# Using the shared product form for the last two missing taps of an input block, and moving VectorE's differences ahead of two groups of additions

## The reference, cut to what matters

```python
# x: (8, 64, 128, 64) = B, C, T, V float32
xp = jnp.pad(x, ((0, 0), (0, 0), (0, 8), (0, 0)), mode='edge')   # time
patches = xp[:, :, idx, :]                 # 16 patches of 16 steps, stride 8
xf = jnp.fft.rfft(patches, axis=-2, norm='ortho')
h = concat(real, imag) @ W.T               # 8 * 64 * 16 = 8192 tokens of 64
...
f = l2norm(h)
attn = softmax(f @ f.T)                    # 8192 x 8192
h = layernorm(h + l2norm(0.8 * f + 0.2 * attn @ f))
h = layernorm(h + moe_top2_of_8(h))        # exact gelu experts
```

## Time and profile before

| | |
|---|---|
| time, median of 3 runs | 855.12 us (854.82 to 855.29) |
| profiled execution: its time, its span | 855.08 us, 853.0 us |
| PE busy | 838.5 us (98%) |
| DVE busy | 781.0 us (92%) |
| ACT busy | 660.0 us (77%) |
| POOL busy | 184.8 us (22%) |
| DMA | 26.09 MB, mean 31 GB/s |

### The profile page before, as it was taken

One profiled execution on the slowest core, in us unless ns is written; L12 is line 12 of the kernel. 1 busy time (PEld: TensorE's weight loads), 2 busy tenths in 40 slices (PEclk: granted clock), 3 DMA queues, 4 the chain that ended last, 5 costly groups with the idle time before them and its releaser, 6 DMA issues.

```text
span 853.0 us, 31799 instructions
## 1 busy us (share of the span) xinstructions
PE 838.5 (98%) x13818; PEld 431.9 (51%) x13818; DVE 781.0 (92%) x920; ACT 660.0 (77%) x1312; POOL 184.8 (22%) x191
## 2 busy tenths in 40 slices
PE   9999999999999999999999999999999999999995
PEld 6444556755555555555555555555555555543331
DVE  4888999999999999999999998999989999999994
ACT  0368888888888888888888888888888888977873
POOL 1275910000400000000000000000000299948323
PEclk9999999999999999999999999999999999999998
DMA  9982150000000000000000000000000000000111
GB/s 297 348 219 59 27 91 3 3 2 2 3 3 3 3 2 3 2 3 2 2 3 2 3 3 3 3 2 3 3 2 3 3 3 3 3 2 2 39 26 37
DMA packets 31578, 26.09 MB, mean 31 GB/s; under 512 B 12552, under 2 KB 29456, under 8 KB 31440
## 3 DMA queue, kind: packets, MB, share of 16 engines
q1 hardware_dynamic: 22912, 15.54, 7.5%
q10 hardware_dynamic: 8464, 8.52, 3.2%
q0 software_dynamic: 64, 0.01, 0.0%
HBM read 17.77 MB, written 2.10 MB: 23 GB/s over the span
## 4 chain that ended last, share of the span: by engine, by line
PE 89%; DVE 6%; DMA 2%; issue 2%; ACT 1%; POOLq 0%; DVEq 0%; POOL 0%; ACTq 0%
PE ps L565 37%; PE ps L582 26%; PE ps L595 12%; PE ps L668 3%; PE ps L752 3%; DVE ring L1101 3%; DMA big<-in_x_dram 2%; PE ps L609 1%; PE ps L473 1%; PE ps L681 1%; PE ps L487 1%; PE ps L767 1%; PE ps L449 0%; DVE ring L1266 0%; DVE sums L1060 0%
## 5 line engine op out<-in xcount | busy, mean ns | idle before, releaser
L1101 DVE TENSOR_TENSOR ring<-ring 128x1024 f16<-128x1024 f32 x512 | 605.0, 1233 | 33.1 <-ACT ring L974 32.1
L974 ACT ACTIVATE ring<-ps 128x1024 f32<-128x1024 f32 x512 | 519.7, 1021 | 120.7 <-PE ps L565 120.5
L565 PE MATMUL ps<-big 64*64 64x512 f16 x6144 | 376.1, 375 | 1.3 <-ACT ring L974 0.9
L582 PE MATMUL ps<-ring,both_f 64*64 64x512 bf16 x4096 | 275.1, 384 | 0.0
L565 PEld LDWEIGHTS ps<-big 64*64 64x64 f16 x6144 | 176.6, 106 | 160.3 <-ACT ring L974 5.5
L582 PEld LDWEIGHTS ps<-ring,both_f 64*64 64x64 f16 x4096 | 119.3, 106 | 106.6
L595 PE MATMUL ps<-ring,both_f 64*64 64x512 f16 x2048 | 154.3, 376 | 0.1
L974 ACT ACTIVATION_READ_ACCUMULATOR ring<-ps 128x1 f32 x512 | 101.3, 198 | 0.0
L393 POOL TENSOR_SCALAR stat<-stat 128x16 f32<-128x16 f32 (+2 forms) x4 | 2.9, 723 | 444.0 <-DVE stat L1150 443.7
L595 PEld LDWEIGHTS ps<-ring,both_f 64*64 64x64 f16 x2048 | 59.8, 107 | 51.8 <-issue 1.9
L937 ACT ACTIVATE ring<-ps,b1s 128x512 f32<-128x512 f32 x64 | 40.4, 683 | 16.7 <-PE ps L668 16.6
(11 more groups left out here) (193 smaller groups left out, 550.4 us busy)
## 6 DMA issues: line engine op xcount, KB each, us to landing
ring<-in_x_dram ACTq DMA_DIRECT2D x6, 1024.0 KB, 15.4
ring<-in_x_dram SPq DMA_DIRECT2D x6, 1024.0 KB, 21.7
big<-big SPq DMA_DIRECT2D x16, 128.0 KB, 2.4
out_dram<-h SPq DMA_DIRECT2D x14, 128.0 KB, 2.4
both_f<-in_x_dram ACTq DMA_DIRECT2D x1, 1024.0 KB, 22.0
both_f<-in_x_dram SPq DMA_DIRECT2D x1, 1024.0 KB, 22.3
big<-in_x_dram SPq DMA_DIRECT2D x1, 1024.0 KB, 24.1
big<-in_x_dram ACTq DMA_DIRECT2D x1, 1024.0 KB, 14.6
```

The costliest lines, as they stand in the source:

```text
L565: last = mm(bank(SLOT_BANK[slot_of(s)] + r)[m:m + 64, :], of_k[r][:, 128 * k + m:128 * k + m + 64], of_q[r][:, q0 + 512 * r:q0 + 512 * r + ...
L582: last = mm(bank(sums_bank(s // NT) + half)[m:m + 64, :], fs[64 * r:64 * r + 64, s % NT, m:m + 64], probs[64 * r:64 * r + 64, s % 8, :].bi ...
L974: a(probs[:, s % 8, :], bank(SLOT_BANK[slot_of(s)], 2), ACT.Exp, accum_out=rowsum[:, s:s + 1]).then_inc(s_pr, 1)
L1101: tt(probs_lo[:, s % 8, :], probs[:, s % 8, :], probs[:, s % 8, :].bitcast(BF16)[:, 1:2 * QC:2], ALU.subtract).then_inc(s_lo, 1)
```

## The change

Blocks 6 and 7 use the shared form in tap 0 too, as blocks 1 to 5 do. In DVE's loop, for `b = 7` all four differences come before `tokens_out(4)` and `tokens_out(5)`, which now follow each other; for `b = 3` and `b = 5` the order is what it was. `norms(4)` follows `tokens_out(5)`.

```diff
-SHARED_TAPS = [()] + 5 * [(0, 1, 2, 3)] + 2 * [(1, 2, 3)]
+SHARED_TAPS = [()] + 7 * [(0, 1, 2, 3)]
...
             for b in (3, 5, 7):
                 taps = SHARED_TAPS[b]
-                for s in taps[:-2]:
+                ahead = 2 if b < B - 1 else len(taps)
+                for s in taps[:ahead]:
                     differences_of(b, s)
                 tokens_out(b - 3)
-                differences_of(b, taps[-2])
+                for s in taps[ahead:-1]:
+                    differences_of(b, s)
                 tokens_out(b - 2)
-                differences_of(b, taps[-1])
+                if b < B - 1:
+                    differences_of(b, taps[-1])
                 norms(b - 3)
                 if b < B - 1:
                     taps = SHARED_TAPS[b + 1]
                     differences_of(b + 1, taps[0])
                     norms(b - 2)
                     for s in taps[1:]:
                         differences_of(b + 1, s)
```

## The result

Over 19 runs of each kernel the changed one has a median of 857.16 us and the one before 855.29 us. The ratio is 1.0025 with a 95% interval of 1.0016 to 1.0034: 2.1 us slower, 1.4 to 2.9. The forecast of 855.8 us was 1.4 us too low. The spread has grown as well: runs of the kernel before lie between 854.2 and 856.6 us, runs of the changed one between 854.8 and 860.9. The profiled execution is one of the longest: 860.51 us, 5.43 more than the profiled one before. This execution shows the case that the prediction called rival A (everything behind block 7 held up through POOL), with one more cost on top.

What follows compares the result with a forecast made beforehand. PE was taken to bound the kernel, with DVE's low parts setting its pace from 68 to 79 us. Block 7's edge +0.5 and a theft +0.2 added to 855.08 gave 855.8 us; range 854.6 to 858.8.

Steps and rivals of the forecast that it cites:

- rival A: POOL's maximum of group 3 starved until block 7's differences end, copy of block 7 late: +3.5 us, 858.6; chance 0.18 in full.
- +0.5 at the edge of block 7: DVE's differences delay PE in block 6, so block 7 ends on PE at 65.05 instead of 64.54.
- theft of the first low part: POOL's work for the norms of group 4 ends about 69.0, delaying DVE's first low part: 0.2 us, between 0 and 0.97.
- rival B: No POOL hit on (6,3), differences ahead of PE: block 7's edge at 63.9, -0.6 us, 854.4 to 854.5; chance 0.08.
- it should hit (6,3): POOL's subtraction for group 1 goes in at block 6's tap 3 difference on DVE, costing 0.97 us; it ends at 57.33.
- tap 3 of block 6 at 56.8 or earlier: On PE, a start of this tap by 56.8 us would show the prediction wrong; it expected near 57.4.
- A's sign for the profile: POOL's line 358 at about 5.6 us, ACT's scalings from 63.7, copy of block 7 starting long after PE's edge.
- Tap 3: not before 57.38: Block 6's last tap on PE waits for its difference, delayed by POOL's theft; edge at 58.73 against 57.29.
- the likeness with 99.38: Similarly spaced POOL request elsewhere: the maximum of group 3 still ends at 57.43, the power takes 2.48 instead of 1.67.
- 0.6 us of slack: ACT could start the copy of block 7 at 64.7, while PE allows it only at 65.36.
- `low_part(7)` sets PE's pace: DVE's low parts, not PE's own path, decide the low sums' start: 0.5 + 0.2 = +0.7 us.
- The prize: Two full taps in blocks 6 and 7 become shared on PE, 1.72 to 1.29 us each: 0.86 us less work at most.

Runs made afterwards that it cites:

- e8: The changed kernel timed once more, unedited: ratio 1.0020 to the kernel before, twelve runs in two groups with means 855.5 and 859.3 us.
- e4: The changed kernel with the scaling of group 3 moved from ScalarE to POOL and its rounding put behind half tile 2: 857.08 us, ratio 1.0018.
- e5: The changed kernel with six products of zeros on PE between the first scores and tokens 6: 859.26 us, ratio 1.0047.
- e12: The changed kernel with the SyncE half of block 7's load started only when TensorE is done with block 5: 858.34 us, ratio 1.0033.
- experiment 9: Nine profiles compared for when VectorE reached block 7's first difference against that block's load landing, plus kernel e9; counts 43 runs of the changed kernel and e9.
- e3: The changed kernel with VectorE waiting ahead of block 7's differences until POOL's subtraction for group 1 is done: 856.46 us, ratio 1.0010.
- e9: The changed kernel with the SyncE half of block 7's load started after block 4 instead of block 3: 858.55 us, ratio 1.0029.

## Why the prediction was right or wrong

**Direction and mechanism.** Forecast was 855.8 us, 0.7 us slower, with 0.58 for that case and 0.18 for rival A in full. The direction was right, the size was not: the measured 2.1 us are three times as much, and outside the 1.7 us within which the prediction saw no change (it gave 0.74 to a time inside and 0.23 to "slower"). The 2.1 us are a mixture of two cases, and no single execution is typical of them. In e8 seven runs are early (mean 855.5, no slower than before) and five late (859.3), with what A foresaw behind block 7; of the first 19 runs eight were over 858. The range held the time. The likeliest case's own range, 855.3 to 856.5, did not hold the median.

**The early case was close by luck.** The forecast's +0.7 is +0.5 at the edge of block 7 and +0.2 for a theft of the first low part. In e8 the edge is 0.62 us early (63.92 against 64.54), which is rival B's number, 63.9, and the theft, at the second low part, takes its full 0.97:

```profile
67.78 2.17 POOL L370 TENSOR_TENSOR both_f<-both_f 128x512 f16<-128x512 f32 x1
```

The low parts start 0.62 us earlier (67.72 against 68.34), and twelve of them take 16.49 us against 15.52. -0.62 + 0.97 = +0.35: two wrong terms that nearly cancel.

**The step that failed** is where I put POOL's subtraction for group 1: "it should hit (6,3)", as it had hit the instruction in that slot before. It stood there for all executions. In none of the three profiles of this order in which POOL got in at the load (e4, e5, e8) did it hit (6,3); it hit (7,0), one later, and in the first profile of the changed kernel it was let in nowhere. Only e12 has it at (6,3). I had read that block 7 was loaded by 55.15 and that the new order "asks for it later", and took it for harmless. The prediction's own sign of being wrong, tap 3 of block 6 at 56.8 or earlier, came up in e8: 56.30. The table of experiment 9 suggests that the opening at that place hangs on this load, and that coming later than the load closes it; it does not show it. A was argued from the maximum of group 3, which asks later; it was the subtraction ahead of it, in the same queue. A's sign for the profile, line 358 at about 5.6 us, did not come: line 370 took 7.75 and line 358 0.24. B's paragraph had this: "a subtraction refused there stays in POOL's queue and delays the maximum of group 3 behind it, which is A". It got no chance of its own; the 0.18 was for another way into the same delay, which 13 of 31 runs have by their times.

**Point by point, by e8's profile.**

- Block 6 waits for its differences: right. Its tap 0 starts 0.20 us late for DVE, and tap 1 is late too. "Tap 3: not before 57.38": wrong, 56.30; no theft fell on (6,3). Edge of block 6 57.60, not 58.73. Of these 1.13 us, 0.39 were there at tap 0 already (52.04 against 52.43).
- Block 7, no waits: right. Its edge is at 63.92, not 65.05, by the same 1.13 us.
- The power of group 3 with 2.48 us instead of 1.67, and the maximum with 1.2, by the likeness with 99.38: right to 0.02 us in all three profiles.
- "0.6 us of slack" for the copy of block 7: wrong. With an earlier edge and a later POOL, ACT is the late one: the copy starts 0.40 behind the edge, and PE waits 0.20.
- `low_part(7)` sets PE's pace: right. PE waits 0.90 us for it, more than the 0.24 of before; low sums 1 start at 79.81, 0.34 later than before, where I had 0.7. e3, which has no late run, measured +0.8 (0.1 to 1.6).
- A's price: 3.5 us over the kernel before. Measured: the groups are 3.8 apart. The copy was 2.85 us late in both profiles of it, where I had 2.6.
- The half clock was not foreseen. It came in one of the two late profiles and not in the other. Its 1.9 us shrink to 0.7 by low sums 1, since the late profile without it waits 0.90 us for `low_part(7)` instead.
- The prize, 0.86 us less for PE: the shared tap costs 1.29 us as read. It is absorbed in waits for DVE in block 6 and ahead of low sums 1.

## What to carry to other kernels

Where two engines shut each other out of SBUF, the gaps of the busier one are a resource: before you fill one, list what has been getting in there and who is waiting behind it. An engine whose own time doesn't matter (POOL, 22% busy) can still gate another's queue. A wait added on purpose to the busiest engine of a stage can be a gain, since it takes the long case away (e3), which here was 13 of 31 runs. And a single profile shows one case of an order that can fall out two ways: take a second one when the runs spread.

## What the runs showed of the hardware

- A POOL instruction that reads SBUF can be kept out by VectorE instructions with two SBUF inputs for as long as these follow each other: 7.75 us, in which five of them went first that had started after POOL had asked (7.74 us and five in e9). The Trainium skill (page "SBUF — State Buffer", section "Who interferes with whom") has "Whoever issues first gets the shared pair for the whole instruction". The trace agrees on the whole instruction (VectorE's took 2.12 and 2.18 us instead of 1.21) and not on the order.
- It is not always kept out between ready neighbours either (e12 at 54.67, e3 at 60.73). What decides there stays open.
- PE stood for 2.5 us in two executions of nearly the same program; the granted clock fell to 0.51 (the 1.2 GHz level) behind one of them and stayed at 1.00 (2.4 GHz) behind the other. In 15 of the 20 runs over 858 us of experiment 9's count the mean granted clock was 0.993 to 0.995, in the other five 0.996 to 0.998.
